# Grouped causal attention: each F32 score product as three F32R products, with queries and keys split two heads ahead

## The reference, cut to what matters

```python
k = jnp.repeat(k, rep, axis=2)          # rep = 4 query heads share one key head
v = jnp.repeat(v, rep, axis=2)
scores = jnp.einsum('bqhd,bkhd->bhqk', q, k) / math.sqrt(HD)
scores = jnp.where(causal[None, None], scores, jnp.finfo(scores.dtype).min)
attn = jax.nn.softmax(scores, axis=-1)
o = jnp.einsum('bhqk,bkhd->bqhd', attn, v).reshape(Bx, Sx, H * HD)
```

## Time and profile before

| what | value |
|---|---|
| time, median of 3 runs (lowest, highest) | 2376.45 us (2376.41, 2380.89) |
| the profiled execution: time / span | 2378.09 us / 2376.3 us |
| mean granted TensorE clock | 0.888 |
| busy over the span: PE, PEld, DVE, ACT, POOL | 81%, 64%, 69%, 46%, 35% |
| grouped attention: first score / last starts of L455 | 1338.9 us / 1716.2 us |
| exponentials L508, 256 of them | 136.6 us busy |
| row maxima L563, 256 of them | 124.8 us busy |
| scaling on GpSimd L557, 256 of them | 277.1 us busy |

### The profile page before, as it was taken

How to read it: one execution, slowest core, us unless ns; L and a number is a source line. 1 busy time by engine, 2 the same in 40 slices (tenths; PEclk the granted TensorE clock), 3 DMA queues, 4 the chain that set the end, 5 groups by cost and what they waited for, 6 DMA issues and landing times. The chain is left out here.

```text
span 2376.3 us, 41325 instructions
## 1 busy us (share of the span) xinstructions
PE 1930.8 (81%) x12514; PEld 1513.0 (64%) x12514; DVE 1628.2 (69%) x3442; ACT 1081.7 (46%) x2394; POOL 820.1 (35%) x841
## 2 busy tenths in 40 slices
PE   5799854999999469997688699999978329999980
PEld 3455443999999233334466477777778329999980
DVE  5567367888888768883877577777744428888855
ACT  1266412444444116883110277777732027777740
POOL 2134222555555210001355577777700330000005
PEclk9689756999999688998789799999989559999995
DMA  4333001000000051210343432323172355555523
GB/s 142 116 81 87 9 1 36 18 26 26 18 26 0 33 187 48 76 45 6 129 128 92 133 108 92 110 88 114 68 239 101 115 197 201 203 203 217 221 82 97
DMA packets 101072, 232.95 MB, mean 98 GB/s; under 512 B 14520, under 2 KB 40504, under 8 KB 95872
## 3 DMA queue, kind: packets, MB, share of 16 engines
q1 hardware_dynamic: 94464, 218.85, 27.0%
q0 software_dynamic: 3072, 8.39, 1.1%
q10 hardware_dynamic: 3456, 4.72, 0.7%
HBM read 157.73 MB, written 72.88 MB: 97 GB/s over the span
## 5 line engine op out<-in xcount | busy, mean ns | idle before, releaser
L557 POOL TENSOR_SCALAR d_att_probs<-d_att_probs,d_att_rinv 128x128 f32<-128x128 f32 (+3 forms) x256 | 277.1, 1088 | 116.6 <-DVE d_att_rinv L568 116.2
L1432 DVE SCALAR_TENSOR_TENSOR b_acc<-bank,b_gates,b_acc 128x256 f32<-128x256 f32 x512 | 212.3, 477 | 41.5 <-PE bank L1347 41.5
L1400 POOL TENSOR_TENSOR b_moe_act_low<-b_moe_act,b_moe_act_high 128x512 fp32r<-128x512 f32 x136 | 176.6, 1298 | 176.8 <-ACT b_moe_act_high L1377 176.8
L455 PE MATMUL wide<-d_att_k,d_att_q 128*128 128x128 f32 (+3 forms) x512 | 184.3, 443 | 15.9 <-DMA d_att_k<-k_dram 15.9
L2013 PE MATMUL wide<-e_moe_hT_high,e_moe_w_high 128*128 128x256 f32 x644 | 183.4, 285 | 13.1 <-DVE e_moe_w_low L2083 13.1
L508 ACT ACTIVATE d_att_probs<-wide,d_att_nmax 128x128 f32<-128x128 f32 (+3 forms) x256 | 136.6, 533 | 113.1 <-DVE d_att_nmax L563 113.1
L2013 PE MATMUL wide<-e_moe_hT_low,e_moe_w_high 128*128 128x256 f32 x644 | 183.3, 285 | 0.0
L2013 PE MATMUL wide<-e_moe_hT_high,e_moe_w_low 128*128 128x256 f32 x644 | 183.2, 284 | 0.0
L2146 POOL DMA_INDIRECT e_out_got<-y_slots,e_pos x32 | 32.1, 1004 | 394.2 <-PEq L2140 385.0
L910 DVE TENSOR_REDUCE c_att_rmax<-wide 128x2 f32<-128x1024 f32 x128 | 152.6, 1220 | 22.6 <-PE wide L687 21.9
L2083 DVE TENSOR_TENSOR e_moe_w_low<-e_moe_w,e_moe_w_high 128x768 fp32r<-128x768 f32 x161 | 151.2, 953 | 21.1 <-ACT e_moe_w_high L2043 18.6
(11 more groups left out here) (359 smaller groups left out, 6012.0 us busy)
## 6 DMA issues: line engine op xcount, KB each, us to landing
e_moe_w<-in_e_w SPq DMA_DIRECT2D x23, 2688.0 KB, 9.7
q_dram<-d_in_rot SPq DMA_DIRECT2D x64, 256.0 KB, 3.6
d_att_q<-q_dram SPq DMA_DIRECT2D x16, 1024.0 KB, 4.9
o_dram<-d_att_o SPq DMA_DIRECT2D x64, 256.0 KB, 2.0
d_out_oT<-o_dram SPq DMA_DIRECT2D x16, 1024.0 KB, 5.6
b_moe_w<-in_b_w SPq DMA_DIRECT2D x17, 512.0 KB, 3.5
e_moe_h<-h_slots SPq DMA_DIRECT2D x23, 256.0 KB
y_slots<-e_moe_y SPq DMA_DIRECT2D x23, 256.0 KB, 9.5
```

Of the source, the lines that this page charges most:

```text
L455: nc.tensor.matmul(stile[qt], qs[s][:, u, qt * P:(qt + 1) * P], ks[s][:, 0, 0:w], start=True, stop=False)
L557: g.tensor_scalar(tile, tile, rinv[:, j, qt:qt + 1], None, ALU.mult).then_inc(scaled, 1)
L1400: g.tensor_tensor(ap[1][:, u % 4, :], act[:, u % 4, :], ap[0][:, u % 4, :], ALU.subtract).then_inc(act_low, 1)
L1432: nc.vector.scalar_tensor_tensor(out=tile, in0=y, scalar=gate, in1=tile, op0=ALU.mult, op1=ALU.add).then_inc(acc_done, 1)
```

## The change

Each head's queries and each quad's keys are split into a high and a low F32R part, and each score is three F32R products in place of one F32 product. `high_query` (ScalarE cast) and `low_query` (VectorE subtraction) work on head `n + 2` in step `n`: the cast stands behind the exponential of `qt = 1`, the subtraction behind the low probabilities of `qt = 2`. For the first head of a quad (in steps `j = 2` and `j = 6`) the keys' cast and subtraction stand ahead of the queries'. Two heads and the first quad's keys are split ahead of the first step. TensorE's scores wait for `q_low` and `k_low`. SyncE's loads wait for `q_low` (the last query subtraction of the slot's quad before) in place of the scores, and stand at `j` of 0 and 4.

```diff
--- before.py
+++ after.py
@@ -391,6 +391,8 @@
 
         pT = [[sb(f"pT{i}_{part}", [P, NQ, S], F32R) for part in ("high", "low")] for i in range(2)]
         vq = [[sb(f"v{i}_{part}", [P, NQ, GD], F32R) for part in ("high", "low")] for i in range(2)]
+        qp = [[sb(f"q{i}_{part}", [P, S], F32R) for part in ("high", "low")] for i in range(2)]
+        kp = [[sb(f"k{i}_{part}", [P, S], F32R) for part in ("high", "low")] for i in range(2)]
         nmax, rsum, rinv = sb("nmax", [P, 8, NQ]), sb("rsum", [P, 8, NQ]), sb("rinv", [P, 8, NQ])
         o_slot = [sb(f"o{i}", [P, S]) for i in range(2)]
         loaded = [sem("loaded0"), sem("loaded1")]
@@ -398,6 +400,7 @@
         scores_done, max_ready, exp_done, scaled, turned, high_ready, low_ready, v_high, v_low, pv_done, o_ready, rinv_ready, spare = (
             sem(n) for n in ("scores", "max", "exp", "scaled", "turned", "high", "low", "v_high", "v_low", "pv", "o", "rinv", "carry"))
 
+        q_high, q_low, k_high, k_low = (sem(n) for n in ("q_high", "q_low", "k_high", "k_low"))
         stile, ttile = ([c.bank[3 * i + k][:, 0:width[qt]] for qt, k in enumerate((0, 1, 0, 2))] for i in range(2))
         obank = c.bank[6:8]
 
@@ -433,9 +436,9 @@
                 with sp.Fori(1, 8) as m:
                     for j in range(8):
                         store(8 * m + (j - 8), j)
-                        if j in (2, 6):
+                        if j in (0, 4):
                             s = j // 4
-                            sp.wait_ge(scores_done, 32 * m + (16 * s - 16))
+                            sp.wait_ge(q_low, 8 * m + (4 * s - 4))
                             load_quad(2 * m + s, s)
                 for j in range(8):
                     store(56 + j, j)
@@ -447,12 +450,15 @@
                 def scores(m, j, qt, first=False):
                     s, u, w = j // 4, j % 4, width[qt]
                     if u == 0 and qt == 0:
-                        pe.wait_ge(loaded[s], (m + 1) * 32)
+                        pe.wait_ge(k_low, 2 * m + s + 1)
+                    if qt == 0:
+                        pe.wait_ge(q_low, 8 * m + j + 1)
                     if qt == 0 and not first:
                         pe.wait_ge(exp_done, NQ * (8 * m + j) - 1)
                     if qt == 2:
                         pe.wait_ge(exp_done, NQ * (8 * m + j) + 1)
-                    nc.tensor.matmul(stile[qt], qs[s][:, u, qt * P:(qt + 1) * P], ks[s][:, 0, 0:w], start=True, stop=False)
+                    for i, (x, y) in enumerate(PRODUCTS):
+                        nc.tensor.matmul(stile[qt], qp[j % 2][x][:, qt * P:(qt + 1) * P], kp[s][y][:, 0:w], start=(i == 0), stop=False)
 
                     nc.tensor.matmul(stile[qt][:, w - P:w], c.identb[:, :], c.causal[:, :], start=False, stop=True).then_inc(scores_done, 1)
 
@@ -519,6 +525,17 @@
                     hold(a, spare)
                     nc.scalar.copy(vq[s][0][:, :, :], vals[:, bass.ds(quad, 1), :, :].rearrange("p a k d -> p (a k) d")).then_inc(v_high, 1)
 
+                def high_query(m, j, first):
+                    s, u = j // 4, j % 4
+                    if u == 0:
+                        a.wait_ge(loaded[s], (m + 1) * 32)
+                        if not first:
+                            a.wait_ge(scores_done, 32 * m + (16 * s - 16))
+                        nc.scalar.copy(kp[s][0][:, :], ks[s][:, 0, :]).then_inc(k_high, 1)
+                    if not (first and j < 2):
+                        a.wait_ge(scores_done, NQ * (8 * m + j) - NQ)
+                    nc.scalar.copy(qp[j % 2][0][:, :], qs[s][:, u, :]).then_inc(q_high, 1)
+
                 def step(m, j, first, last):
                     n = 8 * m + j
                     for qt in range(NQ):
@@ -526,6 +543,8 @@
                         nc.scalar.copy(by_key(pT[j % 2][0], qt), turned_tile(qt)).then_inc(high_ready, 1)
                         if not (last and j == 7):
                             exponentials(*back(m, j, -1), qt)
+                        if qt == 1 and not (last and j >= 6):
+                            high_query(*back(m, j, -2), first and j < 6)
                         if qt == 0 and not (first and j < 2):
                             keep(*back(m, j, 2))
                     if j == 1:
@@ -533,6 +552,8 @@
                     if j == 5 and not last:
                         high_values(2 * m + 2, 0, 8 * m + 4)
 
+                high_query(0, 0, True)
+                high_query(0, 1, True)
                 high_values(0, 0, None)
                 for qt in range(NQ):
                     exponentials(0, 0, qt)
@@ -572,6 +593,14 @@
                     nc.vector.tensor_tensor(vq[s][1][:, :, :], vals[:, bass.ds(quad, 1), :, :].rearrange("p a k d -> p (a k) d"),
                                             vq[s][0][:, :, :], ALU.subtract).then_inc(v_low, 1)
 
+                def low_query(m, j):
+                    s, u = j // 4, j % 4
+                    if u == 0:
+                        v.wait_ge(k_high, 2 * m + s + 1)
+                        nc.vector.tensor_tensor(kp[s][1][:, :], ks[s][:, 0, :], kp[s][0][:, :], ALU.subtract).then_inc(k_low, 1)
+                    v.wait_ge(q_high, 8 * m + j + 1)
+                    nc.vector.tensor_tensor(qp[j % 2][1][:, :], qs[s][:, u, :], qp[j % 2][0][:, :], ALU.subtract).then_inc(q_low, 1)
+
                 def step(m, j, first, last):
                     for qt in range(NQ):
                         if not (last and j == 7):
@@ -579,6 +608,8 @@
                         v.wait_ge(high_ready, NQ * (8 * m + j) + qt + 1)
                         nc.vector.tensor_tensor(by_key(pT[j % 2][1], qt), turned_tile(qt), by_key(pT[j % 2][0], qt),
                                                 ALU.subtract).then_inc(low_ready, 1)
+                        if qt == 2 and not (last and j >= 6):
+                            low_query(*back(m, j, -2))
                         if not (last and j == 7):
                             reciprocal(*back(m, j, -1), qt)
                     if j == 1:
@@ -586,6 +617,8 @@
                     if j == 5 and not last:
                         low_values(2 * m + 2, 0)
 
+                low_query(0, 0)
+                low_query(0, 1)
                 for qt in range(NQ):
                     negated_max(0, 0, qt)
                 for qt in range(NQ):
```

## The result

The changed kernel takes 2402.98 us in the median of 4 runs (2398.53 to 2409.02), the kernel before 2376.43 (2375.34 to 2380.89). The ratio is 1.011, with a 95% interval of 1.009 to 1.013: slower by 26.5 us.

The account below looks back on a forecast made before the run. TensorE was taken as the bound, with the ScalarE-VectorE chain 0.37 us behind; 47 x 0.20 + 15 x 1.32 + 2.0 - 0.3 = 30.9 us gave a 2407 us median, range 2388 to 2431.

Parts of the forecast that it names:

- The bound and the slack: Stage steps: TensorE binds, the ScalarE-VectorE chain is only 0.37 us behind; the change delays that chain by 0.57.
- The plain step: From one 512-column exponential to the next without key or value split: 5.74 us against 5.54, +0.20 a step.
- The key step: The 15 loop steps that also split keys: one more cast and subtraction, +1.32 us each, about 6.86.
- The subtraction's duration: VectorE's query subtraction: bounds 0.70 and 1.0 us, taken as 0.70 because GpSimd is then idle.
- the margin of 0.06 against GpSimd: GpSimd's scalings end at offset 4.25, the query subtraction starts at 4.31, so 0.06 us keeps them apart.
- Two smaller signs: Signs in the changed profile: new casts 0.61 us long, three 512-column products in about 0.72.
- The start: Ahead of the first step: key cast and subtraction, query subtraction and handovers delay the first score by 2.0 us.
- The sum: Whole kernel: 47 x 0.20 + 15 x 1.32 + 2.0 - 0.3 = 30.9 us slower, 2407 median.
- the collision: Rival: GpSimd and VectorE contend, each of 77 step subtractions takes 0.98, adding 21.6 us: 2429; chance 0.20.
- The drift: Any drift of the 256-column reciprocal would push GpSimd's scaling into the query subtraction; argument for the collision.
- The cheap cast: Rival: cast costs less than its length, low probabilities of 384 stay at 3.53, -0.11 a step: 2387; chance 0.14.
- The faster case: Rival: TensorE stays the bound, splits fall into holes, every split head gains 0.20: 2366; chance 0.06.

Follow-up runs that it names:

- run 2: Kernel before with three F32R products of the same unsplit operands per score, no casts or subtractions: 2359.36 us, ratio 0.9924.
- run 3: Changed kernel without VectorE's subtractions, casts in place, all three products from the high parts: 2370.62 us, ratio 0.9976 to the kernel before.
- run 4: Changed kernel without ScalarE's casts; unsplit queries and keys serve as high parts, subtractions and three products stay: 2377.40 us, ratio 1.0005 to the kernel before.
- run 1: Changed kernel with all casts and subtractions, but each score one F32 product of unsplit operands: 2405.79 us, ratio 1.0121 to the kernel before.
- run 8: Kernel before, F32 scores, value split spread: cast ahead of the 384-column exponential, half subtractions in two steps: 2354.52 us, ratio 0.9901.
- run 12: Kernel before with F32 scores and only its value split spread over steps, third measurement: 2358.45 us, ratio 0.9918.
- run 6: Changed kernel, query and key casts moved ahead of the 512 exponential, query subtraction cut into two 256-column halves: 2386.12 us, ratio 1.0040 to the kernel before.
- run 7: Changed kernel, query casts moved, query subtraction halved, key and value casts and half subtractions spread over steps: 2355.84 us, ratio 0.9910 to the kernel before.
- run 5: Changed kernel, query and key casts moved between 512-column probabilities cast and 512 exponential, queries three heads ahead, four buffers: 2381.96 us, ratio 1.0024 to the kernel before.
- run 9: Against run 7: first query half moved behind the 256-column maximum, key and value halves on GpSimd: 2347.57 us, ratio 0.9880 to the kernel before.
- run 11: Same kernel as run 9, measured again: 2348.23 us, ratio 0.9880 to the kernel before.
- run 10: Kernel before with F32 scores and only its value split spread over steps, second measurement: 2355.10 us, ratio 0.9918.

## Why the prediction was right

The measured 2402.98 lies 4 us under the forecast 2407 and inside its range. Point by point, with what the trace after shows:

- *The bound and the slack.* Confirmed. With the products alone (run 2) the step shrank to 5.30, so TensorE was the bound; with one of the two burdens alone (runs 3 and 4) the step stayed under 5.54, with both it went over. The loss in run 1 without any F32R score shows that it is the splits'. TensorE busy "near 90%" came out as 90.5% of the 120 us.
- *The plain step.* Predicted from 0: cast 2.80, cast of 384 at 3.31, low probabilities 3.84, subtraction 4.31, reciprocal 4.92, maximum 5.02, exponential 5.74. Measured: 2.80, 3.32, 3.85, 4.32, 4.92, 5.00, 5.70. Over the stage it is 5.69, +0.15 for the +0.20 predicted. By this 47 steps lose 2.35 us less than forecast. The overestimate is in the last two terms: the step from reciprocal to maximum is 0.08 and not 0.10, and the maximum takes 0.67 and not 0.69 when it does not have to wait for TensorE.
- *The key step.* Predicted +1.32 over a plain step of before, and key steps of about 6.86 as a sign. No interval of 6.86 is in the trace, because the prediction treated the value split and the key split as if they lay in different steps: both fall between the same two 512 exponentials, and the trace has the one long interval, 8.21, where its terms add up to 5.54 + 1.28 + 1.32 = 8.14. Over the 6.82 of before it is +1.39. The rows of before in that interval, which began at 1500.42:

```profile
1504.61 0.50 ACT L526 CAST d_att_pT_high<-wide 128x384 fp32r<-128x384 f32 x1
...
1506.16 0.16 DVE L568 RECIPROCAL d_att_rinv<-d_att_rsum 128x1 f32<-128x1 f32 x1 [0.28 <-ACT d_att_probs L508]
...
1506.51 0.69 DVE L563 TENSOR_REDUCE d_att_nmax<-wide 128x1 f32<-128x512 f32 x1 [0.18 <-PE wide L457]
```

  Up to the cast of 384 columns (before) and the keys' cast (after) both traces have taken 4.19, so the value split costs the same in both and the +1.39 is the key and query splits'. The delay was foreseen well: 1.69 predicted (1.32 and the slack of 0.37), 1.67 measured: after, the 512 maximum starts 7.51 behind the exponential at 1513.26; before, the reciprocal at 5.74 would have let it start at 5.84. The slack was not: behind a value split the maximum of before starts at 6.09, only 0.25 later than its chain would allow, and not 0.37. The clock stayed at 1.00.
- *The subtraction's duration.* I took 0.70 for the margin of 0.06 against GpSimd; measured it is 0.07 (the three scalings end at 1511.81, the subtraction starts at 1511.88). All 64 lie close together:

```profile
L602 DVE TENSOR_TENSOR d_att_q_low<-d_att_q,d_att_q_high x64: 679/682/685, 1340.9 to 1740.5; 128x512 fp32r<-128x512 f32 x64
```

- *Two smaller signs.* The casts are 0.63 to 0.64 long and not 0.61. The three 512 products take 0.79 from the first one's start to the mask's (1510.96 to 1511.75) and not 0.72; from start to start the others have the 0.23 to 0.24 that was read.
- *The start.* +2.0 predicted, 2.09 measured from the load's landing to the first score; but the load itself landed 0.73 later than in the trace of before. Against this the first interval between 512 exponentials fell from 9.41 to 7.91 us. That this is the change's doing is not shown: with F32 scores the same interval is 8.41 in run 1, 7.60 in run 8 and 8.59 in run 12. It lies where the granted clock is still below 1.00, and that part differs from one execution to another: in the 5 us from 1340 and the 5 us from 1345 it was 0.75 and 0.59 before, 0.50 and 0.83 after.
- *The sum.* 47 x 0.15 + 15 x 1.39 = 27.9 in place of 29.2. Six loop turns cost 0.12 more each (6.11 over 5.69, where they were 5.84 over 5.54), 0.7. With 3.1 later at the first 512 exponential, 1.5 less in the interval behind it, and 0.3 less in the last one (5.18 for 5.52), as it was predicted for the end, that makes 29.9 by hand, and the trace has the last 512 exponential 29.4 us later (1717.65 to 1747.03). The spans differ by 27.5, because what follows took 1.9 us less in this execution. That the change can account for those 1.9 us is not shown. The nearness of 2402.98 to 2407 is therefore in part luck: plain steps too dear by 2.35 and key steps too cheap by 1.05 partly cancel, and so do the later load, the shorter first interval and the shorter rest, which the sum did not have.

The rivals: the collision did not happen in the change, but runs 6 and 7 show that it exists, 0.15 us after a 512-column scaling has started. The drift that was to bring it about would not have: a subtraction that starts 0.67 after the start of a 256-column scaling still takes 0.68 (run 4), so a drift of some hundredths would have cost nothing. The cheap cast is answered by the trace after, where the 384 cast starts at 3.32 and the low probabilities at 3.85, and by run 5, where another place for the same cast gives the step back. The faster case would have needed the splits in holes. Holes enough existed: run 9 found them, on other engines and at other places.

## What to carry to other kernels

Idle time of an engine is not slack. VectorE had a quarter of its time free, in waits of some 0.3 us between links of one chain, and a block of 0.6 us fits into none of them: count the distance from the loop that binds to the next one (here 0.37 us), and see how often a change spends it. Cutting such a block to the size of the waits, or moving it to the one place where its engine really waits, turned the change's loss of 26.5 us into a gain of 7 to 10 over the kernel with F32 scores and the same spread value split (runs 9 and 11 against 10 and 12). And look for the same block in the kernel as it is: the value split had stood in the chain all along, at 1.28 us each time.

## What the runs showed of the hardware

A VectorE subtraction with both inputs in SBUF takes 0.41 to 0.42 us for 128x256 and 0.68 for 128x512. When it starts shortly after a 512-column scaling on GpSimd, it takes longer, and the traces say by how much. Two pairs from run 7, scaling and subtraction:

```profile
1377.54 1.57 POOL L586 TENSOR_SCALAR d_att_probs<-d_att_probs,d_att_rinv 128x512 f32<-128x512 f32 x1 [0.43 <-DVE d_att_rinv L597]
...
1377.63 0.87 DVE L608 TENSOR_TENSOR d_att_q_low<-d_att_q,d_att_q_high 128x256 fp32r<-128x256 f32 x1
...
1525.22 1.56 POOL L586 TENSOR_SCALAR d_att_probs<-d_att_probs,d_att_rinv 128x512 f32<-128x512 f32 x1 [0.43 <-DVE d_att_rinv L597]
...
1525.77 0.42 DVE L608 TENSOR_TENSOR d_att_q_low<-d_att_q,d_att_q_high 128x256 fp32r<-128x256 f32 x1
```

| subtraction | starts after the scaling's start | lasts | ends after the scaling's start | run, start |
|---|---|---|---|---|
| 256 columns | 0.09 | 0.87 | 0.96 | 7, 1377.63 |
| 256 columns | 0.16 | 0.80 | 0.96 | 6, 1500.60 |
| 256 columns | 0.27 | 0.70 | 0.96 | 7, 1394.07 |
| 256 columns | 0.36 | 0.60 | 0.96 | 11, 1356.54 |
| 256 columns | 0.55 | 0.42 | 0.97 | 7, 1525.77 |
| 256 columns | 0.92 | 0.41 | 1.33 | 9, 1679.57 |
| 512 columns | 0.14 | 1.09 | 1.23 | before, 1360.39 |
| 512 columns | 0.27 | 0.96 | 1.23 | before, 1454.71 |

Wherever it starts between 0.09 and 0.36, it ends at the same moment: 0.96 to 0.97 after the scaling's start for 256 columns (99 of them in all traces), 1.23 for 512 (120). Less its own length of 0.41 or 0.68, that is 0.55 both times. So the rows look like a subtraction that stands still until the scaling is 0.55 us old and then runs at its usual pace, not like two engines that slow each other down all the while; and 297 subtractions that start 0.55 or more after such a start take 0.41 to 0.42, though the record lets the scaling last 1.56 to 1.57. It is the scaling's beginning that collides. Beside a 256-column scaling, subtractions of either length that started 0.51 or more after it kept their length (runs 1, 4, 5, 6, 7, 9 and 11). It can also be GpSimd that pays: the first value subtraction of the kernel before starts 0.02 after a 256-column scaling and takes 0.69, and the scaling takes 1.43, where 0.93 is usual (1510.57 in the same trace).

The same wait is in the kernel before: all its value subtractions but the first start 0.14 to 0.27 after GpSimd's 512-column scaling and last 0.96 to 1.09 for 0.68, which is part of the 1.28 that each value split costs. The Trainium skill, GPSIMD Engine Reference, section Key points, has the shared SBUF interfaces; these rows agree with it for the first 0.55 us of a scaling of 512 columns and show nothing of it in the rest.

A narrow F32R product gains nothing: for 128 columns the rows have 0.11 from start to start, so three of them take 0.33, where the F32 pair holds TensorE for 0.22 (1512.68 to 1512.90 in the kernel before). That the score part still gained 0.24 us a step (run 2, 5.54 to 5.30) must then come from the wider tiles.
